# Three experts on all tokens in the head, one at the end, sixty sparse in thirty pairs, where it was four, two and fifty-eight

## The chip, the core and the metric

The kernel runs on one core of a Trainium2 chip. The metric is the time on the device of one execution, in microseconds (us), as the median of several runs. TensorE (PE in the profile) multiplies matrices, VectorE (DVE) and ScalarE (ACT) work element by element, GpSimd (POOL) does small arithmetic and issues the indirect transfers, SyncE (SP) issues the plain transfers.

## What is computed

The reference is a chain of eight blocks on 1024 tokens of 256 numbers. The change touches the last one, a mixture of 64 experts of which each token uses 8:

```python
x = hidden_states.reshape(-1, h)
router_logits = x @ gate_w
routing_weights, selected = jax.lax.top_k(router_logits, K)          # K = 8 of E = 64
routing_weights = jax.nn.softmax(routing_weights, axis=-1)
...
gate = jax.lax.ragged_dot(hidden_sorted, gate_proj_w, group_sizes)
up = jax.lax.ragged_dot(hidden_sorted, up_proj_w, group_sizes)
down = jax.lax.ragged_dot(jax.nn.silu(gate) * up, down_proj_w, group_sizes)
...
out = jnp.sum(out * routing_weights[..., None], axis=1)
```

The hidden width of an expert is 96.

## The kernel before

**Two ways to run an expert.** A dense expert is run on all 1024 tokens, and its result is added with the token's weight, which is zero where the token did not choose it. A sparse expert is run on its own tokens alone, which lie in 192 places (CAP) of a buffer in device memory. FIRST (4) dense experts run in `head`, 58 sparse ones and then the last two dense ones (from LAST = 62 on) in `few`. `expert(n)` says which expert of the reference stands n-th. In `every`, which runs only if some expert has more than 192 tokens, all are dense; it doesn't run with these inputs.

**Numbers in two parts.** Each product of float32 matrices is made of three matmuls (`mm3`, lines 349 to 351) on a rounded part ("high") and the rest ("low"). For each expert ScalarE copies the weights `w7f` into `w7h` (L3175) and VectorE subtracts to get `w7l` (L3180). For the first FIRST experts GpSimd makes the low part (L3186), in the attention stage that runs ahead of the head.

**The head** (`head`). A run is one expert on one half of the tokens, 512 of them; there are nd = 2 * FIRST = 8, first all experts on the first half, then all on the second (`of`). On TensorE a run is `tensor_up` (12 matmuls of 512 columns, 6 for gate and 6 for up) and, two steps later, `tensor_down` (12 matmuls of 256 columns, in two units j of 6). Only three banks take results of `tensor_down`, so unit n waits until VectorE has added unit n - 3 to X (`vector_add`, L3496, four adds for a run). VectorE also forms `h` (L3467) and `h7l` (L3472) of each run and, between them, the routing of the last quarter of the tokens: top 8, places, weights and `HTl` (L3262), the low part of the transposed tokens, for which the first run of the second half waits (`norm.htl.at(4)` when i == FIRST).

**The scatter.** GpSimd sends each token's row to the buffer `slots_in`, with 64 indirect transfers (L3357); the last 27 stand in the head. `pace` holds every second one until TensorE has come to a certain run; the last waits for down unit 10. SyncE may load the first pair of experts (`xe`, L3665, 432 KB) only when all 64 have landed.

**The sparse stage** (`few`, loop over k). Experts go in pairs. Per expert: 3 transposes of 128 columns (`tensor_turn`, L3707), 12 matmuls of 192 columns, 6 of 256. ScalarE scales the result into `ye` (L3813), and three indirect transfers of GpSimd per pair (L3946) send it to `rows_out`, ordered by token and by rank of the choice. Weights lie in a ring of 12 slots.

**The end.** The last dense runs (nl = 4) are partly interleaved with the last sparse experts: `dense_up(0)` and `dense_up(1)` lie between their downs. SyncE gathers `rows_out` in four parts of 2 MB, rw 3, 2, 1 and 0 (L3689 to L3692), each when the rows of a rank have landed. VectorE sums five of the eight token tiles (L3892, L3896, L3923, L3929), TensorE the other three by matmuls with the identity in plain float32 (`tensor_sum`, L3790 and L3791, after them X itself, L3779 and L3780). ScalarE copies that back (L3841), and the last transfer writes it out (L3698).

```python
    def pace(n):
        k = n // 2 - 3
        if m.slots_used and n % 2 == 0 and k >= 0:
            if k < 2 or k % 2:
                G.wait_ge(*dense.up.at(min(nd, k + 1 if k < 2 else (k + 3) // 2)))
            else:
                G.wait_ge(*dense.down.at(min(2 * nd, k)))
```

## Time and profile before

| what | us |
| --- | --- |
| median of 3 runs | 686.11 (685.12 to 688.25) |
| the profiled execution | 685.7 |
| its span, first to last instruction | 683.0 |
| head, to the first transpose of the sparse stage | 445.5 to 497.9 |
| sparse stage, to the end of its last matmul | 497.9 to 649.8 |
| the end | 649.8 to 683.0 |

The stages are cut by TensorE's own instructions. All other times are measured from the start of the span. Outside of the span lie 2.7 us of the profiled execution. A row of a timeline has the start, the duration, the engine, the line, the operation with its tiles, how many instructions it joins, and in brackets how long the engine had been idle and what released it.

### The profile page before, as it was taken

To read this page: it belongs to the slowest core of one execution; us is meant where nothing else is said; L and a number is where in the kernel's file an instruction comes from. 1 tells how busy PE (TensorE), PEld (TensorE's weight loads), DVE (VectorE), ACT (ScalarE), POOL (GpSimd) and SP (SyncE) were. 2 spreads that over 40 slices of the span, in tenths; PEclk is the share of its full clock that TensorE was granted. 3 is DMA by queue.
4 is the path that set the end of the run, shared out by engine and by line. 5 is a ranking of instruction groups with operands and counts; after the bars stand their busy time and mean duration, and the time that the engine had idled before them with its cause. 6 is when DMAs were issued, how large, how long until landed. Compare 5 with 4: busy or idle time off the path is not lost.

```text
span 683.0 us, 14285 instructions
## 1 busy us (share of the span) xinstructions
PE 609.0 (89%) x4996; PEld 508.8 (74%) x5000; DVE 523.7 (77%) x1534; ACT 428.1 (63%) x1150; POOL 363.0 (53%) x524
## 2 busy tenths in 40 slices
PE   3998979898899879989999999897799989988877
PEld 3977867776589834668888878675599888888764
DVE  6494489989856788687778988778778878878466
ACT  3635578949745368767776666452358878868430
POOL 6615848964600225435543888677405665666620
PEclk9999999999999999999999999999799999999998
DMA  8999023200010050039300112534448878876384
GB/s 318 334 300 300 27 58 106 82 2 1 4 47 1 0 231 1 2 95 368 114 2 10 66 67 83 183 135 154 159 146 280 261 263 292 282 251 216 133 344 168
DMA packets 47701, 100.50 MB, mean 147 GB/s; under 512 B 7390, under 2 KB 27951, under 8 KB 46246
## 3 DMA queue, kind: packets, MB, share of 16 engines
q1 hardware_dynamic: 40374, 82.33, 36.0%
q0 software_dynamic: 7248, 17.18, 6.8%
q8 instruction: 42, 0.69, 0.4%
q14 instruction: 37, 0.30, 0.2%
HBM read 60.04 MB, written 43.12 MB: 151 GB/s over the span
## 4 chain that ended last, share of the span: by engine, by line
PE 59%; DVE 19%; POOL 8%; ACT 7%; issue 6%; another core or an unknown queue 0%; DMA 0%; DVEq 0%; ACTq 0%; POOLq 0%
PE bank L349 13%; PE bank L351 12%; PE bank L350 11%; PE bank L2650 4%; PE bank L3707 3%; PE bank L2668 3%; PE bank L2658 2%; POOL hl L1238 2%; DVE st L382 2%; DVE HN L402 2%; DVE pt L1451 1%; DVE nm L1459 1%; PE bank L3790 1%; PE bank L1574 1%; POOL raw L1329 1%
## 5 line engine op out<-in xcount | busy, mean ns | idle before, releaser
L3946 POOL DMA_INDIRECT rows_out<-ye,di x87 | 91.4, 1051 | 65.0 <-issue 19.3
L3357 POOL DMA_INDIRECT slots_in<-row,si x64 | 65.6, 1026 | 25.1 <-issue 17.2
L349 PE MATMUL bank<-x7h,w7h 128*96 128x192 f32 x232 | 63.0, 272 | 10.5 <-DVE h L3885 5.7
L2839 POOL TENSOR_SCALAR p6n<-p6n,ri6n 128x128 f32<-128x128 f32 x120 | 46.1, 401 | 46.2 <-DVE ri6n L2785 45.8
L349 PE MATMUL bank<-w7h,h7h 96*128 96x256 f32 x164 | 49.7, 303 | 14.8 <-DVE X L3496 9.4
L351 PE MATMUL bank<-x7h,w7l 128*96 128x192 f32 x232 | 59.1, 255 | 0.3 <-issue 0.2
L350 PE MATMUL bank<-x7l,w7h 128*96 128x192 f32 x232 | 59.0, 254 | 0.0
L2715 ACT ACTIVATE p6n<-sc6n,mn6n 128x128 f32<-128x128 f32 x128 | 50.4, 397 | 10.8 <-DVE mn6n L2762 10.4
L396 POOL TENSOR_TENSOR rs<-ve,neghalf 128x2 f32<-128x2 f32 x32 | 23.1, 721 | 59.4 <-DVE ve L390 59.1
L3180 DVE TENSOR_TENSOR w7l<-w7f,w7h 128x640 fp32r<-128x640 f32 x60 | 49.5, 826 | 4.2 <-issue 2.3
L349 PEld LDWEIGHTS bank<-x7h,w7h 128*96 128x96 f32 x232 | 38.0, 164 | 13.9 <-DVE w7l L3180 8.9
L350 PE MATMUL bank<-w7l,h7h 96*128 96x256 f32 x164 | 47.6, 290 | 0.8 <-issue 0.8
L3803 ACT CAST x7h<-bank 128x384 fp32r<-128x384 f32 x58 | 27.8, 482 | 32.5 <-PE bank L3707 28.7
L351 PE MATMUL bank<-w7h,h7l 96*128 96x256 f32 x164 | 47.7, 291 | 0.0
L3175 ACT CAST w7h<-w7f 128x640 fp32r<-128x640 f32 x64 | 47.2, 740 | 0.0
L349 PEld LDWEIGHTS bank<-w7h,h7h 96*128 96x128 f32 x164 | 32.3, 197 | 16.5 <-DVE X L3496 7.7
L3813 ACT ACTIVATE ye<-bank,wd 128x256 f32<-128x256 f32 x87 | 38.8, 485 | 8.9 <-PE bank L351 7.0
L3846 DVE TENSOR_TENSOR x7l<-bank,x7h 128x384 fp32r<-128x384 f32 x58 | 31.7, 548 | 16.1 <-ACT x7h L3803 14.0
L2762 DVE CUSTOM_DVE_ANT_0 sc6n<-bank,nm 128x128 f32<-128x128 f32 x128 | 29.4, 285 | 13.6 <-PE bank L2650 13.6
L351 PEld LDWEIGHTS bank<-x7h,w7l 128*96 128x96 f32 x232 | 38.0, 164 | 0.3 <-issue 0.3
L350 PEld LDWEIGHTS bank<-x7l,w7h 128*96 128x96 f32 x232 | 38.1, 164 | 0.0
L1441 ACT ACTIVATE p<-bank,nm 128x256 f32<-128x256 f32 x64 | 29.6, 483 | 9.4 <-DVE nm L1459 9.2
(483 smaller groups left out, 2247.0 us busy)
## 6 DMA issues: line engine op xcount, KB each, us to landing
w7f<-in_w SPq DMA_DIRECT2D x64, 320.0 KB
xe<-slots_in SPq DMA_DIRECT2D x29, 432.0 KB
slots_in<-zt SPq DMA_DIRECT2D x7, 1728.0 KB, 17.9
rows_out<-zt SPq DMA_DIRECT2D x8, 1024.0 KB, 11.1
rw<-rows_out SPq DMA_DIRECT2D x3, 2048.0 KB
w0raw<-in_w SPq DMA_DIRECT2D x3, 768.0 KB
wo<-in_w_o SPq DMA_DIRECT2D x1, 2048.0 KB
raw<-in_w SPq DMA_DIRECT2D x2, 704.0 KB
```

The lines of the kernel that those rows point to most:

```text
L349: T.matmul(out, lh, rh, start=first, stop=False, **kw)
L350: T.matmul(out, lh, rl, start=False, stop=False, **kw)
L351: return T.matmul(out, ll, rh, start=False, stop=last, **kw)
L1441: a = A.activation(m.p2[n][:, mc, :], B[2 * (k % 2) + i % 2][:, mc * 256:mc * 256 + 256], ACT.Exp, bias=m.nm2[n][:, mc:mc + 1], accum_out= ...
L2715: a = A.activation(m.p6n[q % 5][:, i, :], m.sc6n[q % 3][:, i, :], ACT.Exp, bias=m.mn6n[q % 5][:, i:i + 1], scale=-1.0, accum_out=m.su6n[q ...
L2839: a = G.tensor_scalar(p, p, m.ri6n[q % 5][:, i:i + 1], 1.0, ALU.mult, ALU.mult)
L3175: A.copy(self.high(e)[:], self.whole(e)).then_inc(self.hi.sem, 1)
L3180: V.tensor_tensor(self.low(e)[:], self.whole(e), self.high(e)[:].bitcast(F32), ALU.subtract).then_inc(self.lo_v.sem, 1)
L3357: G.indirect_dma_start(out=m.buf_in, out_offset=bass.IndirectOffsetOnAxis(ap=m.si7[:, t, j:j + 1], axis=0), in_=m.row7[:, t, :], in_offset ...
L3813: A.activation(m.ye7[q % NY][:], out_bank(q), ACT.Copy, scale=m.wd7[:, 0, q:q + 1]).then_inc(ye.sem, 1)
L3846: V.tensor_tensor(m.x7l[j % 3][:, c, :], B[c][:, 0:2 * CAP], m.x7h[j % 3][:, c, :].bitcast(F32), ALU.subtract).then_inc(xl.sem, 1)
L3946: G.indirect_dma_start(out=m.buf_out, out_offset=bass.IndirectOffsetOnAxis(ap=m.di7[:, q:q + 1], axis=0), in_=m.ye7[q % NY][:], in_offset= ...
```

## The change

FIRST goes from 4 to 3 and LAST from 62 to 63. The head then has 6 runs where it had 8, the sparse stage 30 pairs where it had 29, and 2 dense runs stand at the end where there were 4. The expert that leaves the head loses its copy on ScalarE and its low part on GpSimd in the attention stage ahead of it, and its own buffer. The gathered rows rw 0 and 1 lie one weight slot further on, since the last dense expert's weights are now in slot 0. At the end, TensorE's list for the third and fourth dense run is gone, and VectorE's four sums are spread over the shorter loop.

```diff
-FIRST, LAST = 4, 62
+FIRST, LAST = 3, 63
...
-    a = Room(nc, sixth)
-    m.w7h.append(a("w7h3", [P, 640], F32R))
-    both(m.w7f, m.w7l, a, 3)
...
-    a = Room(nc, rest)
+    a = Room(nc, rest + 5120)
     m.rw7 = [a(f"rw7{i}", [P, NT, 2, D]) for i in range(2)]
...
-            if k in (12, 16, 20, 24):
+            if k in (12, 16, 20):
                 w7.scalar_high(k // 4 - 3)
...
-            if k in (13, 17, 21, 25):
+            if k in (13, 17, 21):
                 w7.gpsimd_low(k // 4 - 3)
...
-        dense_up(2)
-        dense_down(0)
-        dense_up(3)
-        for q in (1, 2, 3):
+        for q in range(nl):
             dense_down(q)
...
-            if k >= 2:
-                vector_sum(nl + 1 - k)
+            if k:
+                vector_sum(4 - k)
+        vector_sum(1)
...
-        value[f"load{s}"] -= 16 * ((E7 - loads) // 8)
+        value[f"load{s}"] -= 16 * len([e for e in range(loads, E7) if e % 8 == s])
```

On TensorE, in the head: `HTh` and `HTl` are the tokens' high and low part, `w7h` and `w7l` an expert's weights, `h7h` and `h7l` the hidden values. Before, behind the down of the first run:

```order
L351 MATMUL bank<-w7h_354,h7l_439 128x256
L349 MATMUL bank<-HTh,w7h_387 96x512 [waits hid,w7_lo_g]
L350 MATMUL bank<-HTl,w7h_387 96x512
L351 MATMUL bank<-HTh,w7l_389 96x512
L349 MATMUL bank<-HTh,w7h_387 96x512
```

With the change, at the same place:

```order
L347 MATMUL bank<-w7h_354,h7l_436 128x256
L345 MATMUL bank<-HTh,w7h_354 96x512 [waits hid,w7_lo_g,normed_T_lo]
L346 MATMUL bank<-HTl,w7h_354 96x512
L347 MATMUL bank<-HTh,w7l_356 96x512
L345 MATMUL bank<-HTh,w7h_354 96x512
```

The fourth up is no longer that of a fourth expert on the first half but the first one on the second half, and the wait for `HTl` of the last quarter (normed_T_lo) has moved from the fifth up to the fourth. (The changed file has four lines fewer ahead of this.)

On VectorE, at the end: `rw_466`, `rw_465`, `rw_464`, `rw_463` are the parts 3, 2, 1 and 0 of the gathered rows. Before, from the sum of part 3 on:

```order
L3892 TENSOR_TENSOR rw_466<-rw_466 128x5x256 [waits load3]
L3467 TENSOR_TENSOR h_433<-bank,sg_430 96x512 [waits gate]
L3472 TENSOR_TENSOR h7l_439<-h_433,h7h_436 96x512 [waits hid_hi]
L3496 SCALAR_TENSOR_TENSOR X<-bank,wt_365,X 128x256 [waits x,down]
L3496 SCALAR_TENSOR_TENSOR X<-bank,wt_365,X 128x256 [waits x]
L3496 SCALAR_TENSOR_TENSOR X<-bank,wt_365,X 128x256 [waits x,down]
L3496 SCALAR_TENSOR_TENSOR X<-bank,wt_365,X 128x256 [waits x]
L3892 TENSOR_TENSOR rw_465<-rw_465 128x5x256 [waits load2]
L3896 TENSOR_TENSOR rw_466<-rw_466,rw_465 128x5x256 [waits rows_sum]
```

With the change, where `rw_463` is part 3 and `rw_460` part 0:

```order
L3885 TENSOR_TENSOR rw_463<-rw_463 128x5x256 [waits load3]
L3492 SCALAR_TENSOR_TENSOR X<-bank,wt_365,X 128x256 [waits down]
L3492 SCALAR_TENSOR_TENSOR X<-bank,wt_365,X 128x256
L3492 SCALAR_TENSOR_TENSOR X<-bank,wt_365,X 128x256 [waits down]
L3492 SCALAR_TENSOR_TENSOR X<-bank,wt_365,X 128x256
L3885 TENSOR_TENSOR rw_462<-rw_462 128x5x256 [waits load2]
L3889 TENSOR_TENSOR rw_463<-rw_463,rw_462 128x5x256 [waits rows_sum]
L3885 TENSOR_TENSOR rw_461<-rw_461 128x5x256 [waits load1]
L3889 TENSOR_TENSOR rw_463<-rw_463,rw_461 128x5x256 [waits rows_sum]
```

One run's `h`, `h7l` and adds are gone between the sums of parts 3 and 2, and the adds of the other stand ahead of part 3.

## Rows read from the trace of the kernel before

**Rows 1.** Busy time by stage; columns as named, then granted TensorE clock, DMA share, GB/s
```profile
445.50:497.90 52.40, 42.98 (x245) 34.26 (x246) 39.15 (x101) 19.34 (x31) 30.83 (x30) 0.90 0.48 161
497.90:649.80 151.90, 137.85 (x1256) 131.76 (x1254) 116.55 (x307) 115.56 (x311) 87.41 (x88) 0.99 0.71 235
649.80:683.00 33.20, 25.00 (x109) 17.51 (x108) 23.42 (x33) 6.60 (x14) 4.91 (x5) 0.93 0.65 252
```

**Rows 2.** Timeline of TensorE in the head
```profile
456.71 0.37 PE L349 MATMUL bank<-w7h,h7h 96*128 96x256 f32 x1
...
458.23 0.40 PE L349 MATMUL bank<-HTh,w7h 128*96 128x512 f32 x1
...
461.02 0.28 PE L349 MATMUL bank<-w7h,h7h 96*128 96x256 f32 x1
...
464.87 0.38 PE L349 MATMUL bank<-w7h,h7h 96*128 96x256 f32 x1 [2.98 <-DVE X L3496]
...
497.93 0.82 PE L3707 MATMUL bank<-ident,xe 128*128 128x128 f32 x6
```

**Rows 3.** Timeline of VectorE in the head: HTl of the last quarter, and h
```profile
462.75 0.68 DVE L3262 TENSOR_TENSOR HTl<-hT,HTh 128x512 fp32r<-128x512 f32 x1
...
465.52 0.68 DVE L3467 TENSOR_TENSOR h<-bank,sg 96x512 f32<-96x512 f32 x1
```

**Rows 4.** Timeline of GpSimd in the head: the last scatters
```profile
474.20 0.96 POOL L3357 DMA_INDIRECT slots_in<-row,si  x1 [0.30 <-issue]
476.56 0.96 POOL L3357 DMA_INDIRECT slots_in<-row,si  x1 [1.40 <-remote]
...
485.42 0.96 POOL L3357 DMA_INDIRECT slots_in<-row,si  x1 [0.31 <-issue]
488.33 0.96 POOL L3357 DMA_INDIRECT slots_in<-row,si  x1 [1.95 <-PE bank L351]
```

**Rows 5.** Timeline of SyncE's queue: the first loads of pairs
```profile
490.83 14.33 SPq L3665 DMA_DIRECT2D xe<-slots_in  x7
```

**Rows 6.** Transfers from 490 to 496 us, GB/s in 40 slices of 0.15 us
```profile
GB/s 276 246 0 0 0 0 0 0 0 0 0 23 138 276 138 253 207 300 369 415 369 300 415 392 346 392 369 369 415 415 369 184 253 300 346 276 323 392 207 207
```

**Rows 7.** Busy time by stretch: waits of TensorE, and stretches at the lower clock
```profile
461.90:464.80 2.90, 0.00 (x0) 0.00 (x0) 2.79 (x9) 0.00 (x0) 2.29 (x3) 1.00 0.66 218
...
490.70:497.50 6.80, 5.00 (x23) 5.00 (x24) 4.88 (x11) 2.12 (x4) 0.00 (x0) 0.50 0.81 269
...
663.90:667.30 3.40, 3.04 (x13) 2.64 (x14) 3.37 (x7) 0.00 (x0) 0.00 (x0) 0.63 0.97 357
```

**Rows 8.** Timeline of SyncE's queue: loads of pairs, twenty pairs apart
```profile
514.54 0.39 SPq L3665 DMA_DIRECT2D xe<-slots_in  x1
...
615.13 0.39 SPq L3665 DMA_DIRECT2D xe<-slots_in  x1
```

**Rows 9.** Timeline of SyncE's queue: parts 2 and 0 of the gather, the last output
```profile
652.30 0.33 SPq L3689 DMA_DIRECT2D rw<-rows_out  x1
...
662.32 0.48 SPq L3692 DMA_DIRECT2D rw<-rows_out  x1
...
680.09 0.33 SPq L3698 DMA_DIRECT2D out<-X  x1
```

**Rows 10.** Transfers from 652 to 672 us, GB/s in 40 slices of 0.5 us
```profile
GB/s 74 0 459 131 74 500 496 262 459 393 467 197 492 467 270 299 564 500 500 426 377 295 492 524 492 242 352 328 389 348 328 410 315 377 422 455 283 86 25 0
```

**Rows 11.** Timeline of TensorE and ScalarE at the end
```profile
666.57 1.85 PE L3790 MATMUL bank<-rw,ident 128*128 128x512 f32 x2
...
678.57 0.59 PE L3791 MATMUL bank<-rw,ident 128*128 128x256 f32 x2
...
679.47 0.59 ACT L3841 COPY X<-bank 128x512 f32<-128x512 f32 x1
```

**Rows 12.** Timeline of VectorE at the end
```profile
674.64 1.48 DVE L3892 TENSOR_TENSOR rw<-rw 128x1280 f32<-128x1280 f32 x1
676.16 1.56 DVE L3929 TENSOR_TENSOR X<-X,rw 128x768 f32<-128x768 f32 x2
```

More of the change, by code:

```diff
@@ L282, in memory @@
     assert a.at <= rest
-    a = Room(nc, sixth)
-    m.w7h.append(a("w7h3", [P, 640], F32R))
-    both(m.w7f, m.w7l, a, 3)
-    assert a.at <= seventh
     a = Room(nc, top)
@@ L306, in memory @@
     assert a.at <= top + 5120
-    a = Room(nc, rest)
+    a = Room(nc, rest + 5120)
     m.rw7 = [a(f"rw7{i}", [P, NT, 2, D]) for i in range(2)]
-    assert a.at <= rest + 7 * 5120
+    assert a.at <= rest + 8 * 5120
     a = Room(nc, rest + NW * 5120 + 12 * 2048)
@@ L3035, in scalar @@
                     r.scalar_high(g)
-            if k in (12, 16, 20, 24):
+            if k in (12, 16, 20):
                 w7.scalar_high(k // 4 - 3)
@@ L3125, in gpsimd @@
                 i.then_inc(pn.sem, 1)
-            if k in (13, 17, 21, 25):
+            if k in (13, 17, 21):
                 w7.gpsimd_low(k // 4 - 3)
```

## The prediction

> **What bounds the kernel now.** I read the busy time by stage first: head 52.4 us, sparse stage 151.9, end 33.2; TensorE is the busiest engine in each, with 43.0, 137.9 and 25.0 us [rows 1]. Its busy times overlap, so a unit of work is better read from starts. In the head, 12 down matmuls take 458.23 - 456.71 = 1.52 us and 12 up matmuls 461.02 - 458.23 = 2.79, so a dense run costs TensorE 4.3 us and a dense expert 8.6 [rows 2]. Then I looked, at each border, for what the next stage really waits for, since taking work from TensorE pays only down to the next wait. There are two such borders.
>
> Into the sparse stage: TensorE goes without a pause from its last down to the first transpose at 497.93 [rows 2]. The load of the pair that it transposes was issued at 490.83 [rows 5], and the transfers start again at 490 + 11 x 0.15 = 491.65; summing the slices, 432 KB have passed at about 493.4 [rows 6]. So the data waited 4.5 us for TensorE. That slack is all that the head can gain unless the scatters end earlier as well.
>
> Into the output: TensorE's sums of gathered rows run from 666.57 to 679.16, ScalarE's copy ends at 680.06, the last output is issued at 680.09 and the span ends 2.9 us later [rows 9, 11]. The data of part 0 are in by 671.0, 38 slices of 0.5 us behind 652 [rows 10]. Here too TensorE is late, by some 6 us, since the sums stand behind four dense runs in its queue.
>
> **The head.** Removed are two runs: 8.6 us of TensorE, and on VectorE two h, two h7l and eight adds, about 2 x 0.6 + 2 x 0.6 + 8 x 0.4 = 5.6 us by the spacing of such rows (an estimate; the one h shown is 0.68 us with its overlap [rows 3]). Added is a wait. The fourth up now needs HTl of the last quarter, which ends at 462.75 + 0.68 = 463.4 [rows 3], while TensorE is ready at 456.71 + 1.52 = 458.2: 5.2 us idle, where before it had 2.8 us of up work and 0.7 of down and then idled 2.98 us for VectorE until 464.87 [rows 2]. Queued behind are all later runs. VectorE's h of that run stood at 465.52 [rows 3]; it now follows an up that ends at 463.5 + 2.8 = 466.3 and ScalarE's silu of it (some 1.3 us with its signals, an estimate), so it starts at about 467.6, and the adds behind it in VectorE's order start 2 us later. Followed run by run with these costs, TensorE's last down ends near 486 (485 to 489) instead of 497.9.
>
> That is more than the data allow. The scatters in the head are issued 1.27 us apart when nothing holds them. Two waits of the pace show among the last nine: 1.40 us at 476.56 and 1.95 at 488.33, each with 0.30 of normal gap in it [rows 4]. The first is for down unit 6, the second for down unit 10; with one up fewer ahead of it, unit 10 should be signalled near 484. Without both waits the last scatter goes out at 488.33 - 1.10 - 1.65 = 485.6. From there to the load of the first pair it was 490.83 - 488.33 = 2.5 us [rows 4, 5] and to its data 2.6 [rows 6], so TensorE's first transpose can start at 490.9: a gain of 7.0. It is bounded below by the case that unit 10 comes no earlier (4.5, the slack above) and above by TensorE's own 12.
>
> Against that stands the clock. TensorE now idles from 486 to 491. Before, it was granted the lower level, 1.2 GHz, for 6.8 us from 490.7 to 497.5, after idle stretches from 486.8 on, and was back at 2.4 GHz when the sparse stage began; after the 2.9 us idle at 461.9 it stayed at 2.4 [rows 7]. The start of the sparse stage is TensorE's work alone, transposes and warming matmuls. If 3 us of it run at the lower level, 1.5 us are lost; between 0 and 3.4 (6.8 us of it). I take 1.5. **Head: -7.0 + 1.5 = -5.5**, bounds -8 and -1.
>
> **The attention stage** loses one copy on ScalarE and one low part on GpSimd. TensorE sets the pace there, and neither is waited for; I count nothing: it is one instruction on each of two engines that do not set that stage's end, so that a gain is bounded by the length of a copy of 640 columns, below 1 us, and nothing is added there that could cost.
>
> **The sparse stage** gets one pair. Loads of pairs are issued at 514.54 and, twenty pairs later, at 615.13: 5.03 us each [rows 8]. TensorE's bare matmuls would take about 4.3, the rest is stalls that come again every few pairs, with the transfers moving 235 GB/s in the mean [rows 1], so a marginal pair should pay them too. The transfers of the pair (its rows, two experts' weights, three scatters) replace none: the same 64 experts' weights are loaded as before. The zeroing of 384 more places in the first stages runs beside other work. **+5.0**, bounds 4.3 and 5.6.
>
> **The end** loses the other two runs. I anchor at T0, the end of the last sparse down at 649.8, as everything that gathers hangs on it: part 2 is issued at 652.30 = T0 + 2.5 and the last part at 662.32, when the last rows have landed [rows 9]. From 652.3 to 671.0 the transfers hardly stop, at some 260 to 560 GB/s [rows 10]; that is the copying of 6.3 MB, which dense work neither hides nor slows. So data are in at T0 + 21.2, and about 0.5 later signalled. TensorE then has only part 0: each 512-column matmul and its 256-column partner repeat every 1.29 us, two of them 2.58 (the four parts and X, nine such pairs and the first slower one, fill 12.6 us [rows 11]). The copies take until 0.9 after it and the output 2.9. End: T0 + 21.7 + 2.6 + 0.9 + 2.9 = T0 + 28.1, against T0 + 33.2 now: -5.1. VectorE is earlier: its part 0 and its last adds take 1.5 + 1.6 us [rows 12], of data that came first. Between the parts TensorE idles 1 to 2.5 us at a time, and before, a wait of the same kind at 661.3 was followed by a mean clock of 0.63 from 663.9 to 667.3 [rows 7]. Parts 1, X and 0 have 1.3 us of slack among them, so one such dip costs about 0.5. **End: -4.6**, bounds -5.1 and +0.1 (all of parts 1, X and 0 at half speed, 5.2 us).
>
> A rule of the skill bears on this term. The trace gives 18.7 us from the issue of part 2 to the last data [rows 9, 10]. The Trainium skill, DMA: Bandwidth & Descriptors, section "Anatomy of one DMA — SWDGE (gpsimd) path", fits a transfer by about 2.0 us plus its bytes over 436 GB/s; that would be 16.4 us for 6.3 MB, and by it the sum would come out 2.3 us lower. The trace disagrees, since scatters share the engines, and its duration is used.
>
> **The sum** on the profiled execution: -5.5 + 0 + 5.0 - 4.6 = -5.1 us, 685.7 to 680.6. The median shown is 0.4 above that execution, so 686.1 to 681.0.
>
> **Rivals.** (a) *The scatters don't move.* Down unit 10 was signalled late before: GpSimd was released at 488.33 [rows 4], long after the matmuls of that unit stand in the trace. If the same lag returns, the load is issued at 490.8 again, the head gains 4.5 - 1.5 = 3.0, and the time is 686.1 - 3.0 + 5.0 - 4.6 = 683.5. For it: VectorE's adds, which unit 10 needs, are delayed by 2 us through the new wait. Against: one up less stands ahead of it. (b) *The clock takes it back*, the case that ends slower than before. The places are the first microseconds of the sparse stage and the last sums, both now behind idle stretches. At the lower level through all of them the head gives -7.0 + 3.4 and the end +0.1: -3.6 + 5.0 + 0.1 = +1.5, 687.6. It decides against the change once the two losses together exceed 7.1 us. For it: the granted clock of 0.50 for 6.8 us after short idles [rows 7]; against it: 2.9 us idle at 461.9 cost nothing. The Trainium skill, TensorE: Matmul & The Clock Gate, section "What's actually happening", says that the default state is throttled and activity releases the throttle. By that rule (b) is the outcome wherever TensorE is nearly idle; the trace agrees only in part, with 0.63 behind one such wait. (c) *More is gained.* The extra pair fits in TensorE's 4.3 us and no clock is lost: -7.0 + 4.3 - 5.1 = -7.8, 678.3. (d) *A collision*: part 3's gather or the new pair's transfers meet where they didn't, a marginal pair costs 8 instead of 5 and the gather's start slips 3: +0.9, 687.0.
>
> **How the numbers follow.** Chances: the forecast 0.55 (679 to 683), (a) 0.17, (b) 0.10, (c) 0.13, (d) 0.05. Predicted is the forecast, 681.0. For 8 in 10 the range must hold it, (a) and most of (c), and from the unknown clock some of what lies towards (b): 677.8 to 685.8. A change of 0.5% is 3.4 us, about what a measurement of this kernel can tell from none; faster by more is below 682.7. That holds for most of the forecast (0.47), all of (c) and a little of (a): 0.63. Slower by more, above 689.5, needs (b) or (d) and worse: 0.05. The rest is 0.32.
>
> **What would show it.** In the profile after: the fourth up at about 463.5 with a wait for HTl ahead of it; the last scatter near 485.6, the first pair's load near 488.1 and the first transpose near 491, after an idle stretch of TensorE of several us; 30 pairs at 5.0 us; TensorE idle ahead of its sums of parts 2, 1 and 0, and the last output issued about 3.4 to 4.0 us behind the start of part 0's sum. The prediction is wrong if the first transpose still stands near 494, if a pair costs much other than 5 us, or if the gather's data come later than 21 us behind the last sparse down.

## The result and the profile after

The changed kernel takes 684.65 us in the median (682.41 to 686.59, 20 runs), the kernel before on the same chip 686.96 (683.63 to 690.83, 20 runs): a ratio of 0.9967, 95% interval 0.9952 to 0.9983. That is 2.3 us less, within the 0.5% that I called about the limit of measurement, where I had forecast 5.1 less and faster with a chance of 0.63. The profiled execution took 683.88 us with a span of 680.1, against a span of 683.0 before; 0.8 of these 2.9 us come from further up: the head's first dense up starts at 446.13 before and at 445.37 after.

The busy time by stage, cut at the first transpose, the first sparse up and the end of the last recorded sparse down; columns as in [rows 1]:

```profile
445.50:493.18 47.68, 34.46 (x192) 27.17 (x190) 33.78 (x89) 16.27 (x26) 31.95 (x36) 0.79 0.44 148
493.18:497.50 4.32, 4.32 (x24) 4.32 (x25) 1.12 (x2) 0.99 (x3) 0.00 (x0) 0.58 0.98 348
497.50:648.50 151.00, 138.18 (x1275) 131.92 (x1273) 118.48 (x309) 118.07 (x317) 90.77 (x85) 1.00 0.72 236
648.50:680.10 31.60, 17.73 (x61) 11.92 (x60) 17.62 (x21) 4.80 (x11) 5.23 (x5) 0.80 0.75 290
```

The head is 4.7 us shorter than in [rows 1], its granted clock 0.79 where it was 0.90. Two stretches of the same view were almost wholly at the lower level, 1.2 GHz (a mean of 0.50 is that level throughout):

```profile
460.00:466.90 6.90, 4.18 (x12) 2.84 (x13) 4.70 (x11) 0.58 (x1) 5.11 (x6) 0.56 0.46 155
480.50:497.60 17.10, 10.50 (x52) 10.04 (x52) 9.72 (x22) 4.84 (x9) 7.21 (x12) 0.52 0.62 213
```

The timeline of TensorE, at the fourth up, at the first transpose and first sparse up [rows 2], and at the end, the first sums of parts 1 and 0 [rows 11]:

```profile
462.72 0.74 PE L345 MATMUL bank<-HTh,w7h 128*96 128x512 f32 x1 [5.10 <-DVE HTl L3258]
...
493.18 1.54 PE L3703 MATMUL bank<-ident,xe 128*128 128x128 f32 x6 [3.56 <-DMA xe<-slots_in]
...
497.52 0.33 PE L345 MATMUL bank<-x7h,w7h 128*96 128x192 f32 x1
...
655.08 0.55 PE L345 MATMUL bank<-w7h,h7h 96*128 96x256 f32 x1 [6.56 <-ACT ye L3806]
...
667.19 1.12 PE L3783 MATMUL bank<-rw,ident 128*128 128x512 f32 x2 [1.38 <-DMA rw<-rows_out]
...
672.17 1.12 PE L3783 MATMUL bank<-rw,ident 128*128 128x512 f32 x2 [0.84 <-DMA rw<-rows_out]
```

In the kernel before, the first sparse up stands here (timeline of TensorE):

```profile
500.50 0.33 PE L349 MATMUL bank<-x7h,w7h 128*96 128x192 f32 x1
```

The timeline of GpSimd, where [rows 4] had waits of 1.40 and 1.95 us:

```profile
466.94 0.96 POOL L3353 DMA_INDIRECT slots_in<-row,si  x1 [0.30 <-issue]
469.94 0.96 POOL L3353 DMA_INDIRECT slots_in<-row,si  x1 [2.04 <-PE bank L347]
...
485.58 0.96 POOL L3353 DMA_INDIRECT slots_in<-row,si  x1 [0.31 <-issue]
486.85 1.46 POOL L3353 DMA_INDIRECT slots_in<-row,si  x1 [0.30 <-issue]
```

And the timeline of SyncE's queue, for [rows 5], [rows 8] and [rows 9]:

```profile
489.85 12.33 SPq L3661 DMA_DIRECT2D xe<-slots_in  x7
...
511.56 0.41 SPq L3661 DMA_DIRECT2D xe<-slots_in  x1
...
616.57 1.01 SPq L3661 DMA_DIRECT2D xe<-slots_in  x1
...
664.47 0.43 SPq L3688 DMA_DIRECT2D rw<-rows_out  x1
...
675.94 0.33 SPq L3694 DMA_DIRECT2D out<-X  x1
```

The last rows of ScalarE that scale results into `ye`, two in one row, before and after:

```profile
651.65 0.83 ACT L3813 ACTIVATE ye<-bank,wd 128x256 f32<-128x256 f32 x2
```

```profile
648.21 0.84 ACT L3806 ACTIVATE ye<-bank,wd 128x256 f32<-128x256 f32 x2 [4.37 <-remote]
...
651.14 0.47 ACT L3806 ACTIVATE ye<-bank,wd 128x256 f32<-128x256 f32 x1 [1.61 <-remote]
...
654.09 0.84 ACT L3806 ACTIVATE ye<-bank,wd 128x256 f32<-128x256 f32 x2 [1.98 <-remote]
```

The second of each last pair starts at 652.02 before and at 654.47 after.

The two old pace waits are gone and a new one of 2.04 us stands at 469.94; the first load is issued at 489.85 instead of 490.83 [rows 5]. The first transpose comes at 493.18 instead of 497.93 [rows 2]; of the 4.75 us, 0.8 are from upstream. From there to the first sparse up it takes 4.34 us, where it took 2.57. The last output is issued 3.77 us behind the start of part 0's sum.

### The profile page after: what moved, and what is told of

Read it like the earlier page. It is cut to its first block, busy times and chain, and to the rows that moved or that the text cites. A ratio compares the mean times of both kernels' runs of the same rounds, so it can differ in the third digit from the quotient of the medians.

```text
span 680.1 us, 14163 instructions
## 1 busy us (share of the span) xinstructions
PE 598.3 (88%) x4942; PEld 501.3 (74%) x4946; DVE 515.8 (76%) x1517; ACT 427.3 (63%) x1151; POOL 367.2 (54%) x526
## 4 chain that ended last, share of the span: by engine, by line
PE 51%; DVE 18%; POOL 10%; ACT 8%; issue 6%; DMA 4%; another core or an unknown queue 2%; POOLq 0%; SPq 0%; ACTq 0%; DVEq 0%
PE bank L345 11%; PE bank L347 10%; PE bank L346 9%; PE bank L2646 4%; PE bank L3703 3%; PE bank L2664 3%; PE bank L2654 2%; POOL slots_in L3353 2%; POOL hl L1234 2%; DVE st L378 2%; ACT ye L3806 2%; DVE HN L398 2%; DVE pt L1447 1%; DVE nm L1455 1%
## 5 line engine op out<-in xcount | busy, mean ns | idle before, releaser
L3940 POOL DMA_INDIRECT rows_out<-ye,di x90 | 96.0, 1067 | 69.4 <-ACT ye L3806 23.3
L345 PE MATMUL bank<-x7h,w7h 128*96 128x192 f32 x240 | 64.7, 270 | 11.4 <-DVE w7l L3176 6.8
L2835 POOL TENSOR_SCALAR p6n<-p6n,ri6n 128x128 f32<-128x128 f32 x120 | 45.8, 398 | 47.2 <-DVE ri6n L2781 46.6
L347 PE MATMUL bank<-x7h,w7l 128*96 128x192 f32 x240 | 60.7, 253 | 0.2
L346 PE MATMUL bank<-x7l,w7h 128*96 128x192 f32 x240 | 60.5, 252 | 0.2 <-issue 0.2
L345 PE MATMUL bank<-w7h,h7h 96*128 96x256 f32 x152 | 47.0, 309 | 11.5 <-ACT ye L3806 7.0
L3171 ACT CAST w7h<-w7f 128x640 fp32r<-128x640 f32 x64 | 46.9, 739 | 0.0
L3806 ACT ACTIVATE ye<-bank,wd 128x256 f32<-128x256 f32 x90 | 40.1, 485 | 10.7 <-remote 8.0
L347 PE MATMUL bank<-w7h,h7l 96*128 96x256 f32 x152 | 45.1, 297 | 0.0
L346 PE MATMUL bank<-w7l,h7h 96*128 96x256 f32 x152 | 44.8, 295 | 0.2 <-issue 0.2
L345 PEld LDWEIGHTS bank<-w7h,h7h 96*128 96x128 f32 x152 | 30.6, 202 | 12.9 <-issue 7.3
L2758 DVE CUSTOM_DVE_ANT_0 sc6n<-bank,nm 128x128 f32<-128x128 f32 x128 | 29.4, 285 | 13.9 <-PE bank L2646 13.8
L347 PEld LDWEIGHTS bank<-x7h,w7l 128*96 128x96 f32 x240 | 38.8, 162 | 0.7 <-issue 0.7
```

Of the source, the lines that this page charges most:

```text
L345: T.matmul(out, lh, rh, start=first, stop=False, **kw)
L346: T.matmul(out, lh, rl, start=False, stop=False, **kw)
L347: return T.matmul(out, ll, rh, start=False, stop=last, **kw)
L2835: a = G.tensor_scalar(p, p, m.ri6n[q % 5][:, i:i + 1], 1.0, ALU.mult, ALU.mult)
L3171: A.copy(self.high(e)[:], self.whole(e)).then_inc(self.hi.sem, 1)
L3806: A.activation(m.ye7[q % NY][:], out_bank(q), ACT.Copy, scale=m.wd7[:, 0, q:q + 1]).then_inc(ye.sem, 1)
```

## The experiments

Eighteen kernels ran, on four chips, each beside the kernel before. Executions differ upstream by up to 4 us, so the table counts profiled times from one row, called the reference row below: the first scatter behind the last instruction of GpSimd that writes `rs` (449.47 in the kernel before, 448.69 after). *Load* is the issue of the first pair's load, *turn* the first transpose, both counted from that row; *ramp* is from there to the first sparse up, *sparse* from that to the last scaling ye, *end* from that to the end of the span, and *total* is turn, ramp, sparse and end together. *Median* is that of all runs of the kernel. Each number is rounded by itself, so sums can be off by 0.1. The first two lines are the runs of the section above; their chip is called the first one.

| kernel | load | turn | ramp | sparse | end | total | median | before, same chip |
|---|---|---|---|---|---|---|---|---|
| before, first chip | 41.4 | 48.5 | 2.6 | 151.5 | 30.9 | 233.5 | 686.96 | |
| after, first chip | 41.2 | 44.5 | 4.3 | 156.9 | 25.6 | 231.4 | 684.65 | 686.96 |
| k_before | 39.7 | 43.6 | 2.6 | 129.2 | 32.0 | 207.4 | 656.7 | 657.23 |
| k_after | 39.7 | 43.0 | 4.3 | 133.5 | 33.0 | 213.7 | 663.59 | 657.23 |
| e1_htl_early | 39.2 | 42.5 | 5.0 | 133.5 | 31.1 | 212.1 | 663.23 | 656.58 |
| e2_beats_in_wait | 38.5 | 41.9 | 5.0 | 133.6 | 31.2 | 211.8 | 662.23 | 656.58 |
| e3_beats_at_border | 39.7 | 42.8 | 2.6 | 134.3 | 31.6 | 211.3 | 661.78 | 656.58 |
| e4_no_pace | 37.8 | 41.3 | 2.6 | 133.5 | 32.4 | 209.9 | 662.03 | 656.58 |
| k_after_three | 38.8 | 42.1 | 4.0 | 133.7 | 31.9 | 211.7 | 661.83 | 657.23 |
| k_before_htl | 39.1 | 42.4 | 2.6 | 129.2 | 31.8 | 206.1 | 655.36 | 657.23 |
| g_before_two | 39.2 | 42.6 | 2.6 | 129.2 | 32.2 | 206.6 | 655.48 | 656.58 |
| z_head | 39.8 | 43.0 | 3.0 | 129.2 | 32.2 | 207.4 | 656.71 | 655.77 |
| z_end | 39.8 | 43.2 | 3.0 | 129.2 | 31.7 | 207.1 | 655.96 | 655.77 |
| s_before | 40.7 | 44.7 | 2.6 | 150.9 | 33.2 | 231.5 | 679.31 | 655.77 |
| s_after | 41.4 | 44.7 | 4.1 | 155.9 | 27.8 | 232.5 | 683.17 | 655.77 |
| t_before | 41.6 | 47.2 | 2.6 | 151.9 | 33.9 | 235.6 | 685.33 | 656.58 |
| t_after | 44.8 | 48.2 | 4.0 | 156.9 | 28.6 | 237.7 | 688.83 | 656.58 |
| t_after_three | 40.1 | 43.5 | 4.0 | 156.9 | 27.3 | 231.8 | 682.51 | 656.58 |
| t_after_htl | 46.2 | 49.5 | 5.0 | 160.0 | 27.8 | 242.3 | 693.86 | 683.27 |
| t_after_no_pace | 46.9 | 50.3 | 2.6 | 159.4 | 28.0 | 240.4 | 692.02 | 683.27 |

### Four edits to the changed kernel's head

My theory after the result: the new wait for HTl lowers the clock, the fourth up then runs at half speed, the down unit behind it is late, and the scatters, which the pace holds for that unit, are late with it; the ramp pays for the idle stretch ahead of it. Each kernel takes one link away. e1_htl_early writes the low part of the last quarter's HT ahead of the slot arithmetic:

```diff
         dense.vector_hidden(1, 1)
+        r.vector_low(3)
         r.vector_slots(3, bank)
...
-        r.vector_low(3)
         dense.vector_low(2, 2)
```

> The changed kernel, with VectorE's HTl of the last quarter moved ahead of that quarter's places (it stood after the first tile's row weights). Theory W (the new wait for HTl, and the lower clock behind it, hold down unit 4 and with it the paced scatters): the fourth up starts near 458.5 instead of 462.7 and at 2.4 GHz, no wait of 2.0 us on GpSimd at down unit 4, the last scatter 1 to 2 us earlier, first transpose 1.5 to 2.5 us earlier; 682.0 to 683.0 where the changed kernel has 684.65, ratio to the kernel before 0.993 to 0.995. Rival S (GpSimd's own rate and the landing bound the border, TensorE's wait is hidden): the last scatter moves by under 0.5 us, ratio 0.996 to 0.997.

e2_beats_in_wait fills the wait with matmuls whose result nobody reads:

```diff
             if i == FIRST:
+                beat(T, m, B[7][:, 0:128], 22)
                 T.wait_ge(*norm.htl.at(4))
```

> The changed kernel with 22 warming matmuls on TensorE (0.22 us each, into the free bank 7) ahead of the wait for HTl: the wait stays, only the idle stretch is filled. If the lower clock behind the wait costs by itself: granted clock 1.00 from 460 to 467 instead of 0.56, the fourth up takes 2.8 us instead of 5.1, scatters 1 to 2 us earlier, ratio 0.994 to 0.996. If not (Rival S): ratio 0.996 to 0.998.

e3_beats_at_border puts nine such matmuls ahead of the sparse loop:

```diff
     def tensor():
+        beat(T, m, B[2][:, 0:128], 9)
         for k in range(ns + 12):
```

> The changed kernel with 9 warming matmuls on TensorE ahead of the first transpose, in its idle stretch of 3.6 us. Theory C (the start of the sparse stage loses 1.8 us to the lower clock): transposes and the first up take 2.6 us instead of 4.3, gain 1 to 1.8 us, ratio 0.994 to 0.995. Rival: beats at the lower clock don't bring the clock back in time, ratio 0.996 to 0.998.

e4_no_pace holds scatters only up to the eighth of the head:

```diff
-            pace(n)
+            if n < 8:
+                pace(n)
```

> The changed kernel without the pace's holds from scatter 8 of the head on: GpSimd issues every 1.27 us. Theory: the data of the first pair set the border, so the last scatter near 484.3 instead of 486.85, the load 2.0 to 2.6 us earlier, first transpose earlier by the same, down to TensorE's own end at 489.4: ratio 0.993 to 0.995. Rival: scatters then collide with the weights' loads and land later, or another wait follows at once: ratio 0.996 to 0.998.

All four came out at 661.8 to 663.2 us beside a kernel before of 656.58: ratios of 1.0098 (1.0078 to 1.0118), 1.0081 (1.0062 to 1.0101), 1.0067 (1.0041 to 1.0092) and 1.0087 (1.0064 to 1.0111). This chip runs the kernel before 30 us faster than the first one did, and on it every version of the change was slower than before. The expectations had been written for the first chip, and none of them holds as a ratio to before. What they say of single waits can be read once the changed kernel itself has run on such a chip, so I needed both kernels there.

### Both kernels on the faster kind of chip

> The kernel before, unchanged, once more with a profile, on a chip where it may take some 656 us instead of 687. Of the four variants of the changed kernel, whose times on such a chip were 661.8 to 663.2 against 656.6, we want the kernel before stage by stage beside them. Theory A (a stage that is shorter on this chip in the kernel before has no cover for the changed head): the first transpose of the sparse loop comes only 0 to 2 us later than in the variants (487.0 to 490.2), because the two long down runs of the old head hide less here. Theory B (the end is where it goes): first transpose 5 to 8 us later than in the variants, as on the first chip (497.93 against 493.18), and the time from the last load of gathered rows to the end of the span some 10 us shorter than in the variants.

> The changed kernel, unchanged, beside the kernel before on the same chip. Its ratio on the first chip was 0.9967. If the ratio belongs to the kernel: 0.995 to 0.998. If it belongs to the chip, as the four variants at 1.007 to 1.010 suggest: 1.007 to 1.012, with the first transpose of the sparse loop at 489 to 491 and the profile's clock 0.965 to 0.975 against 0.98 to 0.987 of before.

k_before repeats the kernel before (ratio 0.9994, 0.9978 to 1.001). k_after is slower: 1.0095 (1.0068 to 1.0122). The profiled spans, 654.0 and 660.8, show where: turn -0.6, ramp +1.7, sparse +4.3, end +1.0, and 0.5 upstream. Ratio and places (first transposes at 490.17 and 490.00) are those of the reading that ties the gain to the chip. The extra pair costs what pairs cost here, since their loads are issued 4.28 us apart and not 5.03. What is missing is the gain at either end. For the head, the timelines of GpSimd and SyncE's queue, first of k_before and then of k_after:

```profile
480.79 0.96 POOL L3357 DMA_INDIRECT slots_in<-row,si  x1 [0.30 <-PE bank L351]
482.06 1.43 POOL L3357 DMA_INDIRECT slots_in<-row,si  x1 [0.30 <-issue]
483.80 0.96 POOL L3357 DMA_INDIRECT slots_in<-row,si  x1 [0.31 <-issue]
...
486.31 11.10 SPq L3665 DMA_DIRECT2D xe<-slots_in  x7
```

```profile
482.93 0.96 POOL L3353 DMA_INDIRECT slots_in<-row,si  x1 [0.30 <-issue]
484.20 0.96 POOL L3353 DMA_INDIRECT slots_in<-row,si  x1 [0.30 <-issue]
...
486.70 12.23 SPq L3661 DMA_DIRECT2D xe<-slots_in  x7
```

In k_before the last scatters go out with no wait beyond the issue gap of 0.30, where [rows 4] had 1.40 and 1.95; the first load comes 39.7 us behind the reference row in both kernels. TensorE's first transpose follows 3.9 us behind the load in k_before, where it was 7.1 on the first chip [rows 2, 5]. In k_after, where TensorE waits for the data, it follows 3.3 us behind, so only 0.6 us can be had from TensorE.

With k_after beside them, the four edits can be read too. Their chip is another one of the same kind, so the comparison is of rows, not of medians. In k_after TensorE waits 5.10 us for HTl, the fourth up behind it runs from 460.98 to 466.21 at a clock of 0.50, and the fifteenth scatter from the reference row on, which the pace holds for down unit 4, waits 2.13 us. In e2_beats_in_wait the wait for HTl is still there, but filled; the clock is 1.00 from 456 to 465, the fourth up takes 2.9 us (461.19 to 464.05), and the fifteenth scatter goes out without a wait. That scatter in k_after, then in e2_beats_in_wait (timeline of GpSimd):

```profile
468.28 0.96 POOL L3353 DMA_INDIRECT slots_in<-row,si  x1 [2.13 <-PE bank L347]
```

```profile
466.67 1.89 POOL L3353 DMA_INDIRECT slots_in<-row,si  x1 [0.30 <-issue]
```

So on this kind of chip it is the lower clock behind the wait that holds the scatter, not the wait alone. In e1_htl_early and e4_no_pace that scatter doesn't wait either; in e3_beats_at_border it does, 2.06 us. The load comes earlier than in k_after by 1.1 us in e2_beats_in_wait, 0.5 in e1_htl_early and 1.8 in e4_no_pace, and not at all in e3_beats_at_border. But e2_beats_in_wait and e1_htl_early lose 0.8 in the ramp, which takes 5.0 us behind idle stretches of 4.27 and 7.42 us. In the totals of the table all four are shorter than k_after, by 1.6 to 3.8 us; the ratios to before can't tell them from k_after's. The ramp of e3_beats_at_border is 2.6 instead of 4.3, as its theory said.

For the end, the timeline of SyncE's queue (the last part's loads, then the last output) in k_before and in k_after:

```profile
635.87 0.43 SPq L3692 DMA_DIRECT2D rw<-rows_out  x1
...
651.35 0.33 SPq L3698 DMA_DIRECT2D out<-X  x1
```

```profile
642.85 0.43 SPq L3688 DMA_DIRECT2D rw<-rows_out  x1
...
656.74 0.33 SPq L3694 DMA_DIRECT2D out<-X  x1
```

And the scatters of GpSimd that those loads wait for, again k_before, then k_after:

```profile
627.82 0.98 POOL L3946 DMA_INDIRECT rows_out<-ye,di  x1 [0.31 <-issue]
```

```profile
633.43 0.98 POOL L3940 DMA_INDIRECT rows_out<-ye,di  x1 [0.30 <-issue]
```

The last ye starts at 621.9 and 627.8. The last scatter goes out 5.9 and 5.6 us behind it, and the last load 13.9 and 15.0; on the first chip before, these were 3.4 and 10.3. With pairs 4.28 us apart and three scatters of 1.29 each, GpSimd has a queue when the loop ends. TensorE does its dense runs while that queue drains. In k_before its sums follow them at 637.08 without a wait. Removing two of the runs makes TensorE wait for data instead, 4.55 us ahead of one sum of k_after. The two sums, k_before and k_after:

```profile
637.08 1.91 PE L3790 MATMUL bank<-rw,ident 128*128 128x512 f32 x2
```

```profile
643.08 2.08 PE L3783 MATMUL bank<-rw,ident 128*128 128x512 f32 x2 [4.55 <-DMA rw<-rows_out]
```

From the last load's issue to the end of the span it is 18.1 us in k_before and 17.9 in k_after. That issue alone doesn't set the end: in e4_no_pace it comes only 9.9 us behind the last ye, and the end is 32.4 all the same. The transfers of the four parts keep the DMA engines busy there (a share of 1.00 at 429 GB/s from 635 to 640 in k_before), which makes their own pace the likely bound; no kernel isolates it.

### One part of the change alone

z_end is the kernel before with the last expert of the end cut for TensorE; z_head the same for the fourth expert of the head.

```diff
+            if skim:
+                r = T.matmul(m.B[self.up_banks(i)[part]][0:96, :], wh[:, col], m.HTh[:, c, w], start=True, stop=True)
+                break
             r = mm3(T, m.B[self.up_banks(i)[part]][0:96, :], wh[:, col], wl[:, col], m.HTh[:, c, w], m.HTl[:, c, w],
...
+                if skim:
+                    r = T.matmul(m.B[self.down_bank(i, j)][:, i2 * 256:i2 * 256 + 256], m.h7h[n][:, c],
+                                 wh[0:96, 384:640], start=True, stop=True)
+                    continue
```

> The kernel before with the matmuls of the last expert of the end cut to one in six (up) and one in three (down): it leaves out most of TensorE's work of that expert, and nothing else. That is the part of the change that shortens the end, alone, without the thirtieth pair. TensorE has some 6.5 us less to do there. Theory (on this kind of chip the end waits for the scattered rows and their loads, not for TensorE): 656.7 stays within 1 us, 655.7 to 657.5. Rival (TensorE's work there is on the path, as on the first chip, where the end got 5.3 us shorter): 650 to 653.

> The kernel before with the matmuls of the fourth expert of the head cut in the same way: some 6.5 us less for TensorE in the head, with all scatters, pacing waits and VectorE work left. Theory (the scatters of GpSimd, 1.27 us each without a wait, set when the rows can be loaded): first load of gathered rows still at 486.3, time 655.7 to 658 (a lower clock in the ramp may cost 1 us). Rival (TensorE's runs set it): the load at 483 or earlier, 651 to 654.

z_end came out at 1.0002 (0.9987 to 1.0016), z_head at 1.0008 (0.9994 to 1.0022). Taking some 6.5 us of TensorE's work away changes nothing measurable at either place, as the theory said. The first load stays at 39.8 behind the reference row and the end goes from 32.0 to 31.7. That TensorE's work sets neither border on this kind of chip is shown; that GpSimd's scatters and the transfers set them is read from the waits.

### TensorE slowed on purpose

If the first chip's gain came from TensorE being the late one there, then making it late here should bring it back. A repeated first matmul of a group costs TensorE time and changes no value; dense ups are called with `again=1` and sparse ups with `again=2`:

```diff
-def mm3(T, out, lh, ll, rh, rl, first, last, **kw):
+def mm3(T, out, lh, ll, rh, rl, first, last, again=0, **kw):
+    for _ in range(again if first else 0):
+        T.matmul(out, lh, rh, start=True, stop=True, **kw)
```

> The kernel before with more work for TensorE alone from the head on: each dense up run gets two more matmuls of 128x512 (0.46 us, 11% of its 4.2 us), each sparse up four more of 128x192 (0.36 us, so a pair some 5.0 us where it takes 4.28 on these chips and took 5.03 on the first). The output stays the same. It imitates the first chip, where TensorE's results came later than here. Expected time about 682: 657 and 29 x 0.72 = 21, and 2 to 5 for head and end, if TensorE sets the sparse stage. If GpSimd's scatters (3.9 us a pair) set it, or the data, under 675.

> The changed kernel with the same additions. Theory (the value of the change hangs on whether TensorE is what head and end wait for): against s_before 0.994 to 1.000, where the unchanged pair stands at 1.0095; the first transpose of the sparse loop 3 us or more earlier than in s_before (it was 0.2 us earlier in k_after than in k_before), from the last scaling of expert outputs to the end of the span 3 us or more shorter, a pair 5.0 us more. Rival (something else differs between the chips, transfers or the clock): ratio between the two 1.006 to 1.012, first transposes within 1 us of one another.

s_before came out at 1.036 (1.0338 to 1.0382) of before and s_after at 1.0411 (1.0387 to 1.0434): 679.31 and 683.17, a quotient of 1.0057, below the rival's 1.006 and above the theory's 1.000. The table splits it. The end's gain is back, 33.2 to 27.8 us, as large as on the first chip (30.9 to 25.6). The head's is not: turn is 44.7 in both.

So I slowed the dense runs more (`again=2` in their ups, `again=1` in their downs):

> As s_before, with more again for TensorE in the dense runs: each gets four more matmuls of 128x512 in its up and four of 96x256 in its down (0.92 and 0.48 us, a third of its 4.2 us), the sparse ups as in s_before. The output stays the same. On the first chip the first transpose of the kernel before stood at 497.93, here at 490.2, in s_before at 491.8. Expected: 495 to 499, behind TensorE's own runs with no wait for data, and a time of some 686 to 690.

> The changed kernel with the same additions. Theory (the head's gain is what TensorE comes later than the gathered rows, the end's what it comes later than the scattered ones): first transpose 3 us or more earlier than in t_before, against 0.2 on the unslowed pair and -0.1 in s; end 5 us or more shorter, a pair 5.0 dearer, ramp 1 to 2 us dearer, so 0.994 to 0.999 of t_before, the first chip's 0.9967 among it. Rival (the head never gives anything, since the paced scatters move with TensorE): first transposes within 1.5 us, ratio 1.002 or more.

t_before is 1.0436 (1.0419 to 1.0452), t_after 1.0476 (1.0455 to 1.0498). The end again gives 5.3 us, but the first transpose comes 1.0 us later than in t_before and the quotient of the medians is 1.0051. The rival was right on the head. t_before itself is a little earlier than expected (685.33, first transpose at 492.96). It has 5.6 us from load to first transpose, 2.2 above the data's time, but t_after loses more than that ahead of the load, whose issue moves from 41.6 to 44.8. The timeline of GpSimd in t_after names the wait:

```profile
468.09 0.96 POOL L3355 DMA_INDIRECT slots_in<-row,si  x1 [0.30 <-issue]
471.72 0.95 POOL L3355 DMA_INDIRECT slots_in<-row,si  x1 [2.67 <-PE bank L349]
472.98 1.50 POOL L3355 DMA_INDIRECT slots_in<-row,si  x1 [0.30 <-issue]
```

It is the wait that stood at 469.94 after, on the first chip. In t_before no scatter waits there. Then three of the edits together (e1, e3 and e4), with TensorE slowed in the same way:

> The changed kernel, slowed in the same way, with the three edits of k_after_three: low part of h early, nine beats ahead of the sparse loop, scatters paced only up to the eighth. Theory (what the head gave less than forecast is the wait for that low part, the clock behind it and the scatters held for the late down run): first transpose 2.5 us or more earlier than in t_after, ramp at full clock, 3 to 5 us faster than t_after. Rival: the dense runs themselves are the bound, then the transposes come at the same time and only the ramp gains, 1 to 1.5 us.

t_after_three is 1.0399 (1.0381 to 1.0418) of before, 6.3 us faster than t_after, more than the 3 to 5 expected, and 2.8 faster than t_before. The load moves from 44.8 to 40.1, the first transpose from 48.2 to 43.5. Where TensorE is the later engine, the head's gain exists (47.2 to 43.5), and what eats it in t_after is the new wait together with the pace. The ramp stayed at 4.0 us: the nine matmuls ran as soon as the dense runs ended, and 3.60 us of waiting for the data stood between them and the first transpose, where it was 0.53 in e3_beats_at_border.

Which of the edits does it was to be told by two last kernels:

> The changed kernel, slowed as t_after, with the low part of h early alone. It tells which of the three edits of t_after_three (6.3 us faster than t_after) carried it. Theory A (the wait for the low part starts it: TensorE idle 4.6 us, then the late down run that holds the scatters): this edit alone gives most, 683 to 685.5, first transpose some 42 to 44.5 us behind the first scatter that follows the last group's norm (48.2 in t_after, 43.5 in t_after_three). Theory B (the pace alone holds the scatters): 687 to 689.

> The changed kernel, slowed as t_after, with the scatters paced only up to the eighth and nothing else. Theory A: TensorE still waits 4.6 us for the low part of h and its own runs end late, so the scatters' gain is capped by TensorE: 685.5 to 688. Theory B (the pace is what held the head up): 682 to 685, first transpose 43 to 45 us behind that scatter.

They ran on a chip like the first, with the kernel before at 683.27 (681.51 to 687.24), and no t_after ran beside them. The times that I expected were for the other chip. Of the places, no theory was met: the first transpose comes 49.5 and 50.3 us behind the reference row, where 42 to 45 were expected. 1.0158 (1.0119 to 1.0196) and 1.0135 (1.0094 to 1.0176) can be held against each other alone: their load and turn are alike within 0.8 us, both 6 to 7 us later than with all three edits on the other chip. In t_after_htl the fifteenth scatter waits 0.47 us, where it was 2.67 in t_after, but two later ones wait 1.93 and 3.13 for TensorE; in t_after_no_pace one waits 6.69 for VectorE's rows. The longest wait of each, timeline of GpSimd:

```profile
485.56 1.36 POOL L3355 DMA_INDIRECT slots_in<-row,si  x1 [3.13 <-PE bank L349]
```

```profile
482.48 1.29 POOL L3355 DMA_INDIRECT slots_in<-row,si  x1 [6.69 <-DVE row L3392]
```

Which edit carries t_after_three stays open.

### Versions on the faster chips

> The changed kernel with three of the edits tried one by one: the low part of h ahead of the slots, nine beats of TensorE ahead of the sparse loop, and scatters paced only up to the eighth. Theory (each takes away a part of the head's loss, the clock's and the pace's): first transpose 487 to 489, sparse ups at full clock behind it, 2 to 4 us faster than k_after, ratio to it 0.994 to 0.997. Rival (the loss against before isn't in the head but in the last stage): within 1 us of k_after, 0.9985 to 1.0015 of it.

> The kernel before, with the low part of h for the hidden rows of group 3 written ahead of the slot arithmetic of VectorE, as in e1. Theory (the order of VectorE there is worth little by itself): the kernel before has another up run as cover there, TensorE doesn't wait for it, so ratio 0.998 to 1.002. Rival (the slots are the path to the scatters): they come 1 us later, and with them the sparse loop: ratio 1.001 to 1.003.

> The kernel before, unslowed, with the low part of h early (0.9976 alone) and scatters paced only up to the eighth. Theory: on these chips no scatter of the kernel before waits behind the fourteenth anyway, so the second edit adds nothing, 0.996 to 0.999. Rival: the pacing kept the scatters off VectorE and ScalarE, and without it those are slowed: 1.000 or more.

k_after_three is 1.0084 (1.0064 to 1.0103), 1.8 us or a quotient of 0.9973 below k_after: between theory and rival. The edits give back the head's part, but nothing there pays for the pair (207.4 against 211.7 in the table). k_before_htl, the kernel before with the early low part, is 0.9976 (0.9963 to 0.999), faster than either kernel on this chip; its load comes 0.6 us earlier behind the reference row, its turn 1.2. That is a little better than the theory's 0.998 to 1.002 and against the rival. The same with the pace cut, on another such chip, is 0.9989 (0.9976 to 1.0003), no better, as its theory said. Both gains are below 0.5%.

## Why the prediction was right and wrong

**The end: right in size, wrong in its anchor.** Forecast -4.6; from the last ye to the end of the span it went from 30.9 to 25.6, -5.3, a little beyond the bound of -5.1. TensorE waits for the data of the last parts as forecast, and 3.77 us pass from part 0's sum to the last output's issue (3.4 to 4.0 forecast). But I had hung it on T0, the last recorded sparse down, and by that the forecast's own warning came true: part 0's sum starts at 672.17, 23.7 us behind 648.50, where data within 21 and a signal at 21.7 were forecast. From T0 to the last ye it was 2.2 us before and 6.0 after, so the recorded end of those downs is no anchor: ScalarE takes the last three downs at 648.21, 651.14 and 654.09, 2.9 us apart, while the profile has their matmuls end 2.1 us apart, the last at 648.5. ScalarE's row, which follows their signal, is the better anchor. Cut at T0, the end gives -1.6 and the ramp with the sparse stage +3.4 (151.9 to 155.3), with the same sum. The prediction also set 18.7 us of the trace beside a fit of the Trainium skill, DMA: Bandwidth & Descriptors, section "Anatomy of one DMA — SWDGE (gpsimd) path". That fit is for a single transfer that GpSimd issues. These are SyncE's, and part 0 was issued only at 662.32 [rows 9], so the 18.7 us hold more than the moving of bytes, and they don't show that scatters slowed it. The sum didn't use the fit.

**The extra pair: right.** Forecast +5.0. Loads go from 511.56 to 616.57, 21 pairs in 105.0 us, 5.00 each, where it was 5.03 [rows 8]; first up to last ye grew by 5.4.

**The ramp: right.** Forecast +1.5, measured 4.34 - 2.57 = 1.8 us, at a clock of 0.58. For the last sums no dip came: 1.00 from 663 to 675. It was 0.54 from 651.2 to 661.4, ahead of a wait for the data of part 1, so that little can have been lost by it. e3_beats_at_border and e4_no_pace, in which TensorE's work reaches closer to the first transpose, have ramps of 2.6 us, which is what the higher level gives.

**The head: the step that failed.** "Without both waits the last scatter goes out at 485.6 [...] a gain of 7.0." It had two parts, TensorE's slack of 4.5 us behind the data and 2.5 from earlier scatters. Behind the reference row, the first load came 41.2 us after and 41.4 before: the scatters gave 0.2. The waits of 1.40 and 1.95 did go, but the new wait for HTl, which I had followed along TensorE and VectorE, I had not followed to GpSimd. TensorE idled 5.10 us, the clock was 0.56 in the mean from 460.0 to 466.9, the fourth up took 4.4 us instead of 2.8, and down unit 4 came so late that the pace held a scatter for it, 2.04 us at 469.94. That the clock is the link between the two waits is shown by e2_beats_in_wait on the faster kind of chip, not on this one. Some scatters were longer (1.46 and 1.22 where the row is 0.96) and the load stood 3.0 instead of 2.5 us behind the last one. The slack gave 3.8, as the data took 3.3 us instead of 2.6. So the gain at the first transpose is 4.0 and not 7.0. The wait accounts for 1.7 of the 2.3 us that the scatters lack, the longer rows and the later load for the rest. Rival (a), the scatters that don't move, was the one that held, with 683.5 for its time; its reason, unit 10 signalled late again, was not the cause: the last scatter didn't wait (486.85). That its time came out is luck.

**The sum.** -4.0 + 1.8 + 5.4 - 5.3 = -2.1, with 0.8 upstream the 2.9 of the spans; the medians say 2.3. The 3.0 us between -5.1 and -2.1 are those of the first transpose; ramp, pair and end miss by +0.3, +0.4 and -0.7, which cancel.

**The clock.** In the head, 6.9 us at a mean clock of 0.56 overlap and follow a wait of 5.10 us, and idle stretches of 1.52, 3.04 and 3.56 us lie just ahead of or within the 17.1 us at 0.52, while the last sums kept 1.00 with waits of 1.38 and 0.84 us between them. The Trainium skill, TensorE: Matmul & The Clock Gate, section "What's actually happening", says that the default state is throttled and activity releases the throttle. By it both the head and the last sums should lose; the trace agrees for the head and the ramp and not for the sums. Of rival (b), which had the head's start and the last sums at the lower level throughout, only the ramp came, with 1.8 of its 3.4 us.

**The chip.** What the profile of one chip could not show is that the sign depends on the chip: the same change costs 6.9 us on another (663.59 against 656.7). There the cost is a full pair and a longer ramp, and TensorE isn't late at either border; slowing it brought back the end's gain by itself and the head's only with the three edits. The gain, 0.9967, was measured on the first chip alone; the kernels that ran later on the slower kind were slowed ones.

## What to carry to other kernels

Work taken from an engine pays only as far as the next wait, so at each border read by how much that engine is later than what else the next stage needs; here that was 4.5 and 6 us on one chip and below 1 at both borders on another, and the change gained on the one and lost on the other. A new wait has to be followed to every engine that a signal of the waiting engine paces, not just to the ones that compute with it. And an edit that trades a sure cost (one pair) for slack should be timed on more than one chip before it is kept.

## What the runs showed of the hardware

- Chips differ by 4 to 5% for the same program: the kernel before took 655.8 to 657.2 us on three chips of the faster kind and 683.3 and 687.0 on the slower kind, the latter on the first chip. Of the 29.0 us between the profiled spans (683.0 and 654.0), 22.3 are in the sparse stage, 129.2 us from first up to last ye against 151.5, and 4.9 in the turn. The granted clock in that stage is 1.00 on one and 0.99 on the other [rows 1], so it isn't that.
- On the first chip TensorE isn't always at work in the sparse stage. From 500 to 600 us it is busy 92.8 us in the kernel before, and all of it in k_before, at a clock of 1.00 in both:

```profile
500.00:600.00 100.00, 92.77 (x886) 89.92 (x885) 83.69 (x221) 81.71 (x219) 54.44 (x52) 1.00 0.77 252
```

```profile
500.00:600.00 100.00, 100.00 (x982) 100.00 (x982) 92.98 (x248) 95.89 (x255) 74.30 (x66) 1.00 0.91 305
```

  Some of its pauses end with a row of VectorE, for others the profile names no releaser. The view of its waits from 440 to 690 us has, in the kernel before on the first chip, the following lines (total us, times, longest), 1.3 us in all after, and no such line on the faster one:

```profile
PE bank L349 <- issue: 4.3, 7, 1.4
PE bank L350 <- issue: 0.8, 1, 0.8
PE bank L351 <- issue: 0.2, 1, 0.2
```

  The pauses come at the same places in both kernels: from the third load of a pair in the loop on, loads go out 4.3, 4.6, 6.5, 3.6, 5.0 and 6.2 us apart before and after. Their mean is what makes a pair 5.03 us.
- On that chip TensorE's results also come later than its recorded matmuls end: 5.6 us for the last sparse down of the changed kernel (654.09 against 648.5), where k_after has 0.04 (627.43 against 627.39).
- Matmuls added to a slower chip cost it little in the sparse stage. With 0.72 us more per pair (an estimate from 0.09 us for each of eight matmuls), t_after_htl issued its loads there 5.01 us apart and for 80 us evenly, as t_after did on the faster kind. Without the addition it is 5.03 and uneven on the first chip, and 4.28 on the faster. The whole stage took 160.0 and 159.4 us in the two kernels that ran so, against 156.9 for the changed kernel on the first chip. These are loads of t_after_htl, timeline of SyncE's queue:

```profile
514.45 0.78 SPq L3663 DMA_DIRECT2D xe<-slots_in  x1
...
519.42 0.38 SPq L3663 DMA_DIRECT2D xe<-slots_in  x1
...
524.41 0.42 SPq L3663 DMA_DIRECT2D xe<-slots_in  x1
...
529.43 0.38 SPq L3663 DMA_DIRECT2D xe<-slots_in  x1
```

  So the slower chips aren't slower in each matmul; those of 192 columns start 0.09 us apart on both kinds. What they lack stays open.
- The clock stayed at the lower level while TensorE was working, too: 0.52 over 17.1 us after, in which it was busy 10.5. In t_before, busy 28.0 of 30 us from 460, it was 1.00 throughout and the ramp took 2.6 us:

```profile
460.00:490.00 30.00, 27.96 (x174) 22.61 (x173) 24.89 (x56) 10.47 (x17) 20.30 (x19) 1.00 0.49 157
```
